# Ranking edges inside a tile of 125: 160 accumulating VectorE operations of one tile, or 40 masks of four tiles summed by TensorE

## The chip, the cores and the metric

The kernel runs on one core of a Trainium2 chip. The metric is the device time of one execution in microseconds (us). Engines are named as the profile names them: PE is TensorE, PEld its weight loads, DVE is VectorE, ACT is ScalarE, POOL is GpSimd, SP is SyncE. A name with a q behind it (PEldq, DVEq) is an instruction of that engine's queue that is no work on data: register arithmetic, a branch, a semaphore.

## What is computed

The program is a chain of four graph layers over 1250 nodes and 20000 edges, each followed by a layer norm. Only its skeleton matters here:

```python
edge_index = jnp.stack([src, dst])
x = _layernorm(x + _L0_gnn_ref(x, edge_index_t, 1250, W, b))        # sums over edges by src
x = _layernorm(x + _L1_gnn_ref(x, edge_index, edge_type_8, ...))    # attention, sums by dst
x = _layernorm(x + _L2_gnn_ref(x, src, dst, deg, ...))              # mean by dst
x = _layernorm(x + _L3_gnn_ref(x, edge_index, edge_type_2, ...))    # two relational layers
return x
```

The sums over edges are made with edges sorted by node. So the kernel first sorts the 20000 edges twice: once by `src`, once by `dst`.

## The kernel before

`sort_edges` is called twice in a row at the start of the program, with `name` `src` and then `dst`, and each call has three stages; every stage ends with a barrier of all engines. The first stage counts and ranks, the second turns counts into positions, the third moves the edges there (and multiplies the basis weights of the last layers beside it). Only the first stage is touched.

In it the edges lie as a table of 125 partitions by 160 columns. A column is a tile of 125 edges, 16 tiles (`GT`) are a group, and there are 10 groups (`G`). The node number is split in a high part of 80 values and a low part of 16 values, and each edge becomes a one-hot row of 96. Four engines' loops work on it:

- `build` (DVE) makes the one-hots of a group, in two operations (L293).
- `turn` (PE) transposes the 16 tiles into `pT` (L322) and multiplies 16 times for the counts, into `pC` (L330).
- ACT copies the transposes to SBUF (L353, two copies a group) and the counts (L356, one).
- `compare` (PE) multiplies each transposed one-hot tile by itself into `pE` (L341). The entry for edges i and j of a tile is the number of halves that they share, so it is 2.0 where both have the same node.
- `rank` (DVE) compares such a tile of 125x125 with 2.0, multiplies by the constant mask `earlier` and sums each row with `accum_out`: for each edge the number of earlier edges of its tile with the same node (L307, once per tile, 160 times).

`pE` holds 16 tiles, one group. The order on each engine is fixed by `lagged`, which writes a step i that runs each work on group i minus its lag: on DVE `build(i)`, then `rank(i-2)`; on PE `turn(i)`, then `compare(i-1)`. `peeled` writes the first steps and what is left at the end out one by one, with constant addresses, and puts the steps between in a hardware loop whose addresses and waits are worked out from a register. The number of steps written out ahead of the loop is 1 plus the greatest lag: 3 on DVE, 2 on PE.

Of the kernel before, what the change touches and what calls it, by code (L numbers as in the profile page):

```python
# [19 lines left out]
F32, BF16, I32 = mybir.dt.float32, mybir.dt.bfloat16, mybir.dt.int32  # L20
ALU, ACT, AX = mybir.AluOpType, mybir.ActivationFunctionType, mybir.AxisListType
# [5 lines left out]
EP, T = 125, 160  # L27
GT = 16
# [8 lines left out]
def stage_semaphores(nc, ctx, name):  # L37

    taken = []

    def give_back():
        nc.clear_and_free_semaphores(taken)
        nc.all_engine_barrier(sem_only=True)  # L43

    ctx.callback(give_back)

    def sem(what):
        taken.append(nc.alloc_semaphore(name=f"{name}_{what}_{nc.next_id()}"))
        return taken[-1]

    return sem


def chain(eng, sem):

    count = [0]

    def link(ins):
        count[0] += 1
        ins.then_inc(sem, 1)  # L60
        eng.wait_ge(sem, count[0])

    return link


def wait(eng, sem, value):

    if isinstance(value, int) and value <= 0:
        return
    eng.wait_ge(sem, value)  # L70


def peeled(eng, n, body, first=1, last=0):

    for i in range(first):
        body(i)
    with eng.Fori(first, n - last) as i:  # L77
        body(i)
    for i in range(n - last, n):
        body(i)  # L80
# [6 lines left out]
def lagged(eng, steps, width, works, last=0):  # L87


    most = max(lag for lag, _ in works)  # L90

    def step(i):
        for u in range(width):
            for lag, work in works:
                back = -((u - lag) // width)
                if not (isinstance(i, int) and i < back):
                    work(i - back, u - lag + back * width)

    peeled(eng, steps, step, first=1 + most // width, last=last)
    for n in range(most):  # L100
        for lag, work in works:
            if n < lag:
                at = steps * width + n - lag
                work(at // width, at % width)
# [132 lines left out]
def sort_edges(nc, name, C, identb, key, packed, extra, pair_block, block_f, sorted_out, basis=None):  # L237
# [7 lines left out]
    with ExitStack() as ctx:  # L245
        sb = lambda n, s, d: ctx.enter_context(nc.sbuf_tensor(f"{name}_{n}", s, d))
# [9 lines left out]
        rankin = sb("rank_in_tile", [EP, T], F32)  # L256
# [2 lines left out]
        small = sb("small", [HI, 8], F32)  # L259
        smalli = sb("small_i", [HI, 2], I32)  # L260
        atleast = sb("pair_at_least", [HI, PAIRS], F32)
        eqtmp = sb("eq_tmp", [EP, 4, EP], F32)
        pos_p, pos_s = sb("pos_partition", [EP, T], F32), sb("pos_slot", [EP, T], F32)
        value = sb("packed_value", [EP, T], F32)

# [1 line left out]
        with ExitStack() as c1:  # L267
            sem = stage_semaphores(nc, c1, name)
            pt = c1.enter_context(nc.psum_tensor(f"{name}_pT", [KO, 2, 8, 128], BF16))
            pc = c1.enter_context(nc.psum_tensor(f"{name}_pC", [HI, GT, LO], F32))  # L270
            pe_ = c1.enter_context(nc.psum_tensor(f"{name}_pE", [EP, 4, 4, 128], F32))
            s_dve = sem("dve_chain")
            onehots_ready = sem("onehots_ready")
            transposed, counted, moved = sem("transposed"), sem("counted"), sem("moved")
            compared, ranked = sem("compared"), sem("ranked")
            block = c1.enter_context(nc.Block())

            G = T // GT

            @block.vector  # L280
            def _(v):
                link = chain(v, s_dve)

                link(nc.vector.tensor_copy(ki[:, :], key))
                link(nc.vector.tensor_single_scalar(ti[:, :], ki[:, :], LB, ALU.logical_shift_right))
                link(nc.vector.tensor_copy(hif[:, :], ti[:, :]))
                link(nc.vector.tensor_single_scalar(ti[:, :], ki[:, :], LO - 1, ALU.bitwise_and))
                link(nc.vector.tensor_copy(lof[:, :], ti[:, :]))

                def build(g, _):  # L290

                    for f, iota, a, n in ((hif, "iota_hi", 0, HI), (lof, "iota_lo", HI, LO)):
                        nc.vector.tensor_tensor(  # L293
                            onehot[:, bass.ds(g * GT, GT), a:a + n],
                            C.f(iota, EP).unsqueeze(1).to_broadcast([EP, GT, n]),
                            f[:, bass.ds(g * GT, GT)].unsqueeze(2).to_broadcast([EP, GT, n]), ALU.is_equal,
                        ).then_inc(onehots_ready, 1)

                def rank(g, _):

                    for u in range(GT):
                        if u % 4 == 0:
                            v.wait_ge(compared, g * 4 + (u // 4 + 1))

                        wait(v, ranked, g * GT + (u - 3))

                        nc.vector.scalar_tensor_tensor(  # L307
                            eqtmp[:, u % 4, :], pe_[:, u // 4, u % 4, 0:EP], 2.0,
                            C.f("earlier", EP)[:, 0:EP], ALU.is_equal, ALU.mult,
                            accum_out=rankin[:, bass.ds(g * GT + u, 1)]).then_inc(ranked, 1)  # L310

                lagged(v, G, 1, [(0, build), (2, rank)])

            @block.tensor
            def _(pe):
                def turn(g, _):

                    pe.wait_ge(onehots_ready, g * 2 + 2)

                    wait(pe, moved, g * 3)  # L320
                    for u in range(GT):
                        ins = nc.tensor.transpose(  # L322
                            pt[:, u // 8, u % 8, 0:EP],
                            onehot[:, bass.ds(g * GT + u, 1), :].rearrange("p a n -> p (a n)"),
                            identb[0:EP, 0:EP])
                        if u % 8 == 7:
                            ins.then_inc(transposed, 1)
                    for u in range(GT):
                        oh = onehot[:, bass.ds(g * GT + u, 1), :].rearrange("p a n -> p (a n)")
                        ins = nc.tensor.matmul(pc[:, u, :], oh[:, 0:HI], oh[:, HI:KO],  # L330
                                               start=True, stop=True)
                    ins.then_inc(counted, 1)

                def compare(g, _):

                    pe.wait_ge(moved, g * 3 + 2)
                    for u in range(GT):
                        if u % 4 == 0:
                            wait(pe, ranked, g * GT + (u + 4 - GT))
                        oh = onehotT[:, bass.ds(g * GT + u, 1), :].rearrange("p a n -> p (a n)")  # L340
                        ins = nc.tensor.matmul(pe_[:, u // 4, u % 4, 0:EP], oh, oh, start=True, stop=True)  # L341
                        if u % 4 == 3:
                            ins.then_inc(compared, 1)

                lagged(pe, G, 1, [(0, turn), (1, compare)])

            @block.scalar
            def _(act):

                with act.Fori(0, G) as g:  # L350
                    for w in range(2):
                        act.wait_ge(transposed, g * 2 + (w + 1))
                        nc.scalar.copy(  # L353
                            onehotT[:, bass.ds(g * GT + w * 8, 8), :], pt[:, w, :, 0:EP]).then_inc(moved, 1)
                    act.wait_ge(counted, g + 1)
                    nc.scalar.copy(cnt[:, :, bass.ds(g * GT, GT)].rearrange("p l t -> p t l"),  # L356
                                   pc[:, :, :]).then_inc(moved, 1)


        with ExitStack() as c1:  # L360
            sem = stage_semaphores(nc, c1, name)
# [98 lines left out]
        with ExitStack() as c1:  # L460
            sem = stage_semaphores(nc, c1, name)
# [1009 lines left out]
def gnn(nc, ins, consts, out):  # L1471
# [8 lines left out]
    with ExitStack() as top:  # L1480
# [16 lines left out]
        with ExitStack() as ctx:  # L1497
# [4 lines left out]
            with ExitStack() as c1:  # L1502
# [14 lines left out]
                def _(v):  # L1517
# [7 lines left out]
            f = lambda n: fld[:, n, :]  # L1525
            SH1, SH2 = 8, 19
            sort_edges(nc, "src", C, identb, f(SRC), [(f(DST), 1 << SH1), (f(REL1), 1 << SH2)], None,
                       pairs["src"][:, :], blocks["src"][:, :], [packed["src"][:, :]], basis[1])
            sort_edges(nc, "dst", C, identb, f(DST), [(f(SRC), 1 << SH1), (f(T8), 1 << SH2)], f(WT),
                       pairs["dst"][:, :], blocks["dst"][:, :], [packed["dst"][:, :], weight[:, :]], basis[0])  # L1530

# [231 lines left out]
```

## Time and profile before

| what | value |
|---|---|
| median of 3 runs | 2698.16 us (2689.44 to 2699.32) |
| span of the profiled execution, first to last instruction | 2541.8 us |
| PE busy | 1969.9 us, 78% |
| DVE busy | 1458.9 us, 57% |
| first stage of the sort by src, first key operation to last rank | 10.7 to 90.6 us |
| the same of the sort by dst | 310.2 to 387.5 us |

The profile gives no other time of its own execution than its span, from the first to the last instruction. The run time is the larger by 156 us, which lie outside the instructions. A difference in the span is therefore read as a difference in the run time. Both stages together are some 157 us of the 2541.8, and what they do to the total is read from inside them: the engines are idle there for other reasons than in the rest.

### The profile page before, as it was taken

The numbers are of one execution on the slowest core, as the hardware profiler recorded it, in microseconds if no ns is written. First come the engines' busy times: TensorE is split into PE (matmuls) and PEld (weight loads), VectorE is DVE, ScalarE is ACT, GpSimd is POOL, SyncE is SP. The second block draws the span as 40 slices with busy tenths as digits, with TensorE's granted clock in tenths as the row PEclk, the third lists the DMA queues.
The fourth block names the chain that finished last, engine by engine and source line by source line (L and its number), as shares of the span: only waits on it lengthen the run. The fifth ranks groups of instructions, "written<-read, shape, count | busy, mean of one in ns | idle before, by whom it ended". The sixth has DMA issues, their size and how long they took to land. (4 is left out here: it accounts for less than half of the span.)

```text
span 2541.8 us, 36616 instructions
## 1 busy us (share of the span) xinstructions
PE 1969.9 (78%) x8289; PEld 1126.0 (44%) x8290; DVE 1458.9 (57%) x3550; ACT 479.5 (19%) x889; POOL 976.5 (38%) x974
## 2 busy tenths in 40 slices
PE   7767695885989998558287775699867998888884
PEld 6633385564545554347144442233333333343331
DVE  5644467675257776687677777444453444204445
ACT  4101130111135554223200002100044000120000
POOL 0000000001047771440078773477700777207773
PEclk9988755998989999755599998899989999999998
DMA  0079700998046663000166670577712777317775
GB/s 16 0 160 212 157 0 21 205 206 214 32 117 193 186 191 74 26 0 0 50 176 172 173 183 28 174 208 210 196 36 95 236 209 207 102 66 206 209 208 143
DMA packets 99747, 336.66 MB, mean 132 GB/s; under 512 B 19744, under 2 KB 20369, under 8 KB 95851
## 3 DMA queue, kind: packets, MB, share of 16 engines
q0 software_dynamic: 71904, 235.41, 33.2%
q1 hardware_dynamic: 24714, 96.39, 14.9%
q10 hardware_dynamic: 3072, 4.20, 0.8%
q8 instruction: 24, 0.39, 0.1%
q14 instruction: 33, 0.26, 0.0%
HBM read 310.83 MB, written 25.10 MB: 132 GB/s over the span
## 5 line engine op out<-in xcount | busy, mean ns | idle before, releaser
L658 PE MATMUL e_pS<-e_rows,e_onehot_ring 128*128 128x512 f32 x1408 | 689.4, 617 | 179.9 <-issue 59.7
L578 POOL DMA_INDIRECT e_rows<-tab_y,e_idx_ring x352 | 334.8, 951 | 332.7 <-ACT e_idx_ring L638 226.1
L658 PEld LDWEIGHTS e_pS<-e_rows,e_onehot_ring 128*128 128x128 f32 x1408 | 246.4, 192 | 480.8 <-issue 404.6
L610 DVE TENSOR_TENSOR acc<-e_pS,acc 128x512 f32 x352 | 242.6, 689 | 377.1 <-PE e_pS L658 373.9
L578 POOL DMA_INDIRECT e_rows<-tab_h,e_idx_ring x176 | 205.0, 1165 | 208.1 <-ACT e_idx_ring L638 158.5
L968 PE MATMUL n_pY<-weights,n_xT_block 128*128 128x512 f32 x560 | 260.1, 615 | 0.0
L1583 POOL DMA_DIRECT2D a_in<-in_L_gnn_a_src x1 | 1.0, 966 | 611.0 <-POOLq L43 611.0
L578 POOL DMA_INDIRECT e_rows<-tab_n,e_idx_ring x176 | 167.7, 953 | 77.2 <-issue 49.9
L717 POOL DMA_INDIRECT e_rows<-tab_q,e_idx_ring x176 | 169.8, 965 | 68.1 <-issue 46.4
L792 PE MATMUL e_pS<-e_rows,e_onehot_f 128*128 128x512 f32 x352 | 166.6, 597 | 0.0
L968 PEld LDWEIGHTS n_pY<-weights,n_xT_block 128*128 128x128 f32 x560 | 107.5, 199 | 118.3 <-issue 118.3
L600 DVE TENSOR_TENSOR e_rows<-e_rows,edge_weights 128x1024 f32<-128x1024 f32 x88 | 108.0, 1227 | 67.1 <-DMA e_rows<-tab_h,e_idx_ring 66.5
L214 PE MATMUL basis_ps<-basis_piece,basis_mix 120*32 120x512 f32 x512 | 81.5, 765 | 77.7 <-DMA basis_piece<-in_L_gnn_basis 77.7
L225 ACT COPY basis_wout<-basis_ps 128x512 f32<-128x512 f32 x64 | 37.5, 585 | 410.7 <-PE basis_ps L214 403.4
L507 PE MATMUL dst_pO<-dst_onehot_s,dst_onehot_p 125*128 125x176 f32 x640 | 107.3, 325 | 6.7 <-DVE dst_onehot_s L494 6.7
L736 DVE TENSOR_TENSOR e_rows<-e_rows,e_pP 128x1024 f32<-128x1024 f32 x88 | 107.3, 1219 | 7.8 <-DMA e_rows<-tab_q,e_idx_ring 7.1
L507 PEld LDWEIGHTS dst_pO<-dst_onehot_s,dst_onehot_p 125*128 125x128 f32 x640 | 97.8, 193 | 26.0 <-DVE dst_onehot_s L494 13.2
L661 PEld LDWEIGHTS e_pN<-edge_weights,e_onehot_ring 128*128 128x128 f32 x352 | 67.7, 192 | 85.8 <-issue 85.8
L761 ACT ACTIVATE e_rows<-e_rows 128x1024 f32<-128x1024 f32 x88 | 93.2, 1059 | 5.7 <-DVE e_rows L736 5.7
L745 DVE TENSOR_TENSOR acc<-e_pS,acc 128x512 f32 x88 | 60.8, 691 | 54.9 <-PE e_pS L792 54.9
L489 DVE TENSOR_SCALAR src_onehot_p<-const_table,src_pos_partition 125x128 f32<-125x128 f32 x160 | 44.7, 280 | 82.5 <-PE src_pO L507 82.3
L638 ACT COPY e_idx_ring<-idx_h 128x8 int32 (+1 forms) x44 | 8.5, 197 | 436.7 <-DMA e_rows<-tab_h,e_idx_ring 236.2
(309 smaller groups left out, 3077.4 us busy)
## 6 DMA issues: line engine op xcount, KB each, us to landing
basis_piece<-in_L_gnn_basis SPq DMA_DIRECT2D x128, 480.0 KB, 11.8
tab_y<-n_y_ring SPq DMA_DIRECT2D x40, 256.0 KB, 2.2
e_rows<-tab_y,e_idx_ring POOLq DMA_INDIRECT x352, 3.7
tab_w<-basis_wout ACTq DMA_DIRECT2D x128, 32.0 KB
w_raw<-in_L_gnn_W SPq DMA_DIRECT2D x3, 1024.0 KB, 10.1
weights<-tab_w SPq DMA_DIRECT2D x3, 1024.0 KB, 5.8
e_rows<-tab_q,e_idx_ring POOLq DMA_INDIRECT x176, 3.7
e_rows<-tab_h,e_idx_ring POOLq DMA_INDIRECT x176, 3.8
```

What stands on the lines that cost most here:

```text
L214: ins = self.nc.tensor.matmul(self.ps[32 * q:32 * q + 32, k * 2 + s, :], self.mix[:, :], self.piece[:, k, f:f + D], start=True, stop=True, ...
L507: ins = nc.tensor.matmul(po[:, n, 0:SLOTS], onp[:, u % RING, :], ons[:, u % RING, n, :], start=first and u == 0, stop=last and u == STEP - 1)
L578: pool.indirect_dma_start(rows[:, q, s, :], None, table, bass.IndirectOffsetOnAxis(idxr[:, half, n:n + 1], 0)).then_inc(got[q], 16)
L600: nc.vector.tensor_tensor(r, r, weight[:, bass.ds(i * 16 + u * 2, 2), 0:H].unsqueeze(3).to_broadcast([P, 2, H, DH]), ALU.mult).then_inc(we ...
L610: nc.vector.tensor_tensor(a, pS[:, u % 4, :], a, ALU.add).then_inc(added, 1)
L658: ins = nc.tensor.matmul(pS[:, u % 4, :], ohr[:, u % 4, s, :], rows[:, u, s, :], start=s == 0, stop=s == 1)
L661: ins = nc.tensor.matmul(pN[:, u % 4, 0:ns], ohr[:, u % 4, s, :], weight[:, bass.ds(i * 16 + (u * 2 + s), 1), :].rearrange("p a h -> p (a ...
L717: pool.indirect_dma_start(rows[:, q, s, :], None, q_table, bass.IndirectOffsetOnAxis(idxr[:, half, n:n + 1], 0)).then_inc(got[q], 16)
L736: nc.vector.tensor_tensor(rows[:, u, :, :], rows[:, u, :, :], pP[:, u % 2, :, :], ALU.add).then_inc(summand, 1)
L761: nc.scalar.activation(rows[:, u, :, :], rows[:, u, :, :], ACT.Relu).then_inc(relued, 1)
L792: ins = nc.tensor.matmul(pS[:, u % 2, :], ohf[:, u, s, :], rows[:, u, s, :], start=s == 0, stop=s == 1)
L968: ins = nc.tensor.matmul(py[:, k, w, :], xt[:, k, c, :], weights[w][0][:, c, :], start=c == 0, stop=c == 3)
```

## The change

`rank` on DVE is replaced by two works. `match` on DVE compares a window of four tiles at once (125x500) and writes the masked comparison (0.0 or 1.0) as two-byte numbers into `same`, without summing. A new `rank` on PE multiplies each of the four masks by a column of ones: the mask is the stationary operand, the ones are the moving one, and the result, one column of 125 sums, goes to a new PSUM tile `pR`. After the last group one DVE copy brings `pR` to `rankin`. The step on PE is now `turn(i)`, `compare(i-1)`, `rank(i-2)`; on DVE `build(i)`, `match(i-2)`. The greatest lag on PE goes from 1 to 2. Lines shift: L322, L330 and L341 of before are L324, L332 and L343 of the changed kernel; L307 is the DVE comparison in both.

```diff
-        eqtmp = sb("eq_tmp", [EP, 4, EP], F32)
+        same = sb("same_and_later", [EP, 4, 4, EP], BF16)
+        ones = sb("ones", [EP, 1], BF16)
...
+            pr = c1.enter_context(nc.psum_tensor(f"{name}_pR", [EP, T], F32))
...
+                link(nc.vector.memset(ones[:, :], 1.0))
...
-                def rank(g, _):
-
-                    for u in range(GT):
-                        if u % 4 == 0:
-                            v.wait_ge(compared, g * 4 + (u // 4 + 1))
-
-                        wait(v, ranked, g * GT + (u - 3))
-
+                def match(g, _):
+
+                    for w in range(4):
+                        v.wait_ge(compared, g * 4 + (w + 1))
+                        wait(v, ranked, g * 4 + (w - 3))
                         nc.vector.scalar_tensor_tensor(
-                            eqtmp[:, u % 4, :], pe_[:, u // 4, u % 4, 0:EP], 2.0,
-                            C.f("earlier", EP)[:, 0:EP], ALU.is_equal, ALU.mult,
-                            accum_out=rankin[:, bass.ds(g * GT + u, 1)]).then_inc(ranked, 1)
-
-                lagged(v, G, 1, [(0, build), (2, rank)])
+                            same[:, w, :, :], pe_[:, w, :, 0:EP], 2.0,
+                            C.f("earlier", EP)[:, 0:EP].unsqueeze(1).to_broadcast([EP, 4, EP]),
+                            ALU.is_equal, ALU.mult).then_inc(matched, 1)
+
+                lagged(v, G, 1, [(0, build), (2, match)])
+                v.wait_ge(ranked, 4 * G)
+                nc.vector.tensor_copy(rankin[:, :], pr[:, :])
...
-                            wait(pe, ranked, g * GT + (u + 4 - GT))
+                            wait(pe, matched, g * 4 + (u // 4 - 3))
...
-                lagged(pe, G, 1, [(0, turn), (1, compare)])
+                def rank(g, _):
+
+                    for w in range(4):
+                        pe.wait_ge(matched, g * 4 + (w + 1))
+                        for q in range(4):
+                            ins = nc.tensor.matmul(pr[:, bass.ds(g * GT + (w * 4 + q), 1)], same[:, w, q, :], ones[:, :],
+                                                   start=True, stop=True, skip_group_check=True)
+                        ins.then_inc(ranked, 1)
+
+                lagged(pe, G, 1, [(0, turn), (1, compare), (2, rank)])
```

What PE issues ahead of its loop in the sort by src, before the change (`ISA` is an instruction of the queue that sets registers or waits, the figures at the end are the shape of the result):

```order
L322 MATMUL src_pT<-identb,src_onehot 96x125 x16
L330 MATMUL src_pC<-src_onehot 80x16 x16
L322 MATMUL src_pT<-identb,src_onehot 96x125 x16
L330 MATMUL src_pC<-src_onehot 80x16 x16
L341 MATMUL src_pE<-src_onehotT 125x125 x16
L77 UNCONDITIONAL_BRANCH
```

The same place after the change:

```order
L324 MATMUL src_pT<-identb,src_onehot 96x125 x16
L332 MATMUL src_pC<-src_onehot 80x16 x16
L324 MATMUL src_pT<-identb,src_onehot 96x125 x16
L332 MATMUL src_pC<-src_onehot 80x16 x16
L343 MATMUL src_pE<-src_onehotT 125x125 x16
L324 MATMUL src_pT<-identb,src_onehot 96x125 x16
L332 MATMUL src_pC<-src_onehot 80x16 x16
L343 MATMUL src_pE<-src_onehotT 125x125 x16
L352 MATMUL src_pR<-src_ones,src_same_and_later 125x1 x16
L77 UNCONDITIONAL_BRANCH
```

A whole step, with its `compare` and the first `rank`, has moved out of PE's loop, so that the loop runs 7 times and no longer 8.

The end of PE's loop and what follows it, before the change (each matmul in the loop has an `ISA` of its own ahead of it):

```order
L341 ISA
L341 MATMUL src_pE<-src_onehotT 125x125
L77 REGISTER_ALU
L77 COMPARE_AND_BRANCH
L341 MATMUL src_pE<-src_onehotT 125x125 x16
```

The same place after the change, with the first window of the new `rank`; three more windows like it, each with a `REGISTER_ALU` ahead, stand between the two pieces:

```order
L343 ISA
L343 MATMUL src_pE<-src_onehotT 125x125
L350 ISA
L352 ISA
L352 MATMUL src_pR<-src_ones,src_same_and_later 125x1
...
L77 REGISTER_ALU
L77 COMPARE_AND_BRANCH
L343 MATMUL src_pE<-src_onehotT 125x125 x16
L352 MATMUL src_pR<-src_ones,src_same_and_later 125x1 x32
```

PE's loop body has grown by 16 matmuls, 16 `ISA` of their own and 4 register instructions, and behind the loop stand 32 matmuls more.

## Rows read from the trace of the kernel before

**Rows 1.** The first line of the page of the profile.

```profile
span 2541.8 us, 36616 instructions
```

**Rows 2.** Windows of one loop step: src, dst; x counts instructions, then PEclk, DMA.

```profile
31.98:39.70 7.72, 7.26 (x48) 6.77 (x49) 5.39 (x35) 3.75 (x4) 0.00 (x0) 1.00 0.00 0
328.90:336.71 7.81, 7.31 (x48) 6.80 (x49) 5.68 (x37) 2.57 (x3) 0.00 (x0) 0.50 0.00 1
```

**Rows 3.** Waits, 0 to 95 us: us in total, times, longest.

```profile
DVE src_eq_tmp L307 <- PE src_pE L341: 23.5, 9, 5.0
...
PE src_pT L322 <- ACT src_cnt L356: 2.4, 2, 2.1
...
PEld src_pE L341 <- DVE src_eq_tmp L307: 0.3, 1, 0.3
```

**Rows 4.** Timeline of PE, 20 to 40 us: start, length, operation, count.

```profile
20.64 1.22 PE L330 MATMUL src_pC<-src_onehot 125*80 125x16 bf16 x16
21.71 1.95 PE L341 MATMUL src_pE<-src_onehotT 96*125 96x125 bf16 x16
23.95 2.53 PE L322 MATMUL src_pT<-identb,src_onehot 125*96 125x125 bf16 x16 [0.29 <-ACT src_cnt L356]
...
31.99 2.43 PE L322 MATMUL src_pT<-identb,src_onehot 125*96 125x125 bf16 x16 [0.39 <-issue]
34.23 2.30 PE L330 MATMUL src_pC<-src_onehot 125*80 x16
36.64 2.72 PE L341 MATMUL src_pE<-src_onehotT 96*125 x16
39.70 0.60 PE L322 MATMUL src_pT<-identb,src_onehot 125*96 125x125 bf16 x3 [0.34 <-issue]
```

**Rows 5.** Timeline of all engines, 60 to 125 us: last step, end of stage.

```profile
78.38 2.43 PE L322 MATMUL src_pT<-identb,src_onehot 125*96 125x125 bf16 x16 [0.34 <-issue]
...
85.73 1.35 PEld L341 LDWEIGHTS src_pE<-src_onehotT 96*125 96x125 bf16 x12 [0.16 <-issue]
...
90.55 0.08 DVE L307 DVE_READ_ACCUMULATOR src_eq_tmp<-src_pE,const_table 125x1 f32 x1
91.37 0.06 DVE L376 MEMSET src_small<- 80x1 f32 x1 [0.73 <-PEq L43]
```

**Rows 6.** Source views, 31.9 to 82.9 us: PE's queue; ns min/median/max, starts.

```profile
L330 PEldq FUSED_REGOPS  x112: 55/55/55, 34.1 to 82.6; - x112
...
L341 PEldq FUSED_REGOPS  x96: 55/64/69, 36.5 to 77.6; - x96
...
L77 PEldq COMPARE_BRANCH  x6: 207/208/213, 39.1 to 77.8; - x6
```

**Rows 7.** Timeline of PE, 300 to 392 us, and the last rank of dst.

```profile
321.69 1.89 PE L322 MATMUL dst_pT<-identb,dst_onehot 125*96 125x125 bf16 x16
...
328.90 2.44 PE L322 MATMUL dst_pT<-identb,dst_onehot 125*96 125x125 bf16 x16 [0.34 <-issue]
...
375.29 2.42 PE L322 MATMUL dst_pT<-identb,dst_onehot 125*96 125x125 bf16 x16 [0.35 <-issue]
...
387.43 0.08 DVE L307 DVE_READ_ACCUMULATOR dst_eq_tmp<-dst_pE,const_table 125x1 f32 x1
```

**Rows 8.** Groups by form on DVE, 31.98 to 78.37 us: busy us, mean ns.

```profile
L307 DVE SCALAR_TENSOR_TENSOR src_eq_tmp<-src_pE,const_table 125x125 f32<-125x125 f32 x97 | 22.0, 285 | 12.2 <-PE src_pE L341 12.2
...
L293 DVE TENSOR_TENSOR src_onehot<-const_table,src_hi_f 125x1280 f32 x6 | 9.0, 1493 | 1.5 <-issue 1.5
...
L293 DVE TENSOR_TENSOR src_onehot<-const_table,src_lo_f 125x256 f32 x6 | 2.5, 419 | 0.0
```

**Rows 9.** The page's costliest groups: a DVE operation on 512 columns of PSUM.

```profile
L745 DVE TENSOR_TENSOR acc<-e_pS,acc 128x512 f32 x88 | 60.8, 691 | 54.9 <-PE e_pS L792 54.9
```

**Rows 10.** Timeline of ACT's third group, 0 to 60 us.

```profile
28.75 0.59 ACT L356 COPY src_cnt<-src_pC 80x256 f32 x1 [0.22 <-PE src_pC L330]
```

**Rows 11.** Timeline of PE, 85 to 135 us: the second stage's loop.

```profile
120.95 5.16 PE L451 MATMUL src_pG<-src_prefix_parts,src_onehotT 80*125 x32 [0.33 <-issue]
```

More of the change, by code:

```diff
@@ L274, in sort_edges @@
             transposed, counted, moved = sem("transposed"), sem("counted"), sem("moved")
-            compared, ranked = sem("compared"), sem("ranked")
+            compared, matched, ranked = sem("compared"), sem("matched"), sem("ranked")
+            pr = c1.enter_context(nc.psum_tensor(f"{name}_pR", [EP, T], F32))
             block = c1.enter_context(nc.Block())
```

## The prediction

> **What bounds the stage now.** The chain on the page's foot covers only the program's last microseconds, so I read the two ranking stages from inside. First the windows of one loop step. In the sort by src a step takes 7.72 us, of which PE is busy 7.26 and DVE 5.39 [rows 2]. The step repeats: `turn(3)` starts at 31.99 and `turn(9)` at 78.38, which is 46.39 us for six steps, 7.73 each [rows 4, 5]. Then the waits: DVE waits 23.5 us for PE's `pE`, while PE's loads wait 0.3 us for DVE in the whole stage [rows 3]. So PE sets the pace and DVE, from which the change takes work, is the engine that waits.
>
> Next, what holds PE. Ahead of the loop, with constant addresses, the 16 count matmuls start at 20.64 and the next work at 21.71: 1.07 us, 67 ns each. In the loop the same 16 take from 34.23 to 36.64, 2.41 us to the next work, and the 16 transposes from 31.99 to 34.23: 2.24 us, 140 ns each [rows 4]. The difference stands in PE's queue: ahead of each of these matmuls one register instruction of 55 ns, and at the end of each step a branch of 208 ns [rows 6]. The clock is not it: in the sort by dst the granted clock is 0.50, the lower of the two levels (1.2 GHz), in src it is 1.00 (2.4 GHz), and the step takes 7.81 us against 7.72 [rows 2]. So PE's queue bounds the loop by the number of its instructions, whatever their size. A matmul of one column costs there what one of 125 does.
>
> **What the change does to a loop step.** It removes 16 DVE operations of 227 ns each (22.0 us over 97), 3.6 us, and adds four of 500 columns out of PSUM. The nearest row is a DVE operation on 512 columns of PSUM, 691 ns [rows 8, 9]; a bit less, 0.68 us, gives 2.7 us. With `build` (1.49 and 0.42) DVE then has 4.6 us in a step. I cost these edits at nothing: they lie beside PE's work both before and after. This cover goes only if DVE needed more than PE's step.
>
> It adds to PE 16 matmuls, 16 register instructions of their own and four waits. Neither is in the trace, so I bound their cost. From below: 16 pairs at the loop's 140 ns, 2.24 us. From above: `compare` is built alike, 16 pairs with four waits; from its start at 36.64 to the next `turn` at 39.70 are 3.06 us, and without the branch (0.21) 2.85, in which `turn`'s own two waits are counted too [rows 4, 6]. The new pairs have one changing address like the transposes, so I go between, 2.6 us. PE's idle time in a step, 0.46 us [rows 2], offers no cover, since its queue is at work then. **A step becomes 7.73 + 2.6 = 10.33 us.**
>
> Here the Trainium skill speaks of another price. "TensorE: Matmul & The Clock Gate", section "Back-to-back issue gap", gives about 81 ns for a sustained pair of weight load and matmul of 128 columns. By that figure the new `rank` would take 16 x 81 ns = 1.3 us, a step 9.0 us, and the total would rise by some 17 us and not by 35. The trace agrees with it roughly for the matmuls that are written out (67 ns) and not for those in the loop (140 ns).
>
> **New waits.** `match(i-2)` waits on `compare(i-2)`, and, window by window, on `rank(i-3)`, both of PE's previous step. PE needs it only for `rank(i-2)`, behind `turn(i)` and `compare(i-1)`, some 7.3 us later; DVE needs 2.7 us for it and 1.9 for the next `build`. Behind a late `match` on DVE only that `build` is queued, and PE's `turn` would wait for it; it has some 5 us to spare. `compare` now waits on `matched` of the group before, which comes earlier than `ranked` did.
>
> **The step that leaves the loop.** With a lag of 2 PE writes out three steps and loops over seven. In src `turn(2)` starts at 23.95 either way, released by ACT [rows 4]. Written out, it costs 1.7 us for transposes (105 ns each, an estimate between the 67 and 140 ns above) and 1.07 for counts, `compare(1)` 1.9 [rows 4], `rank(0)` 16 x 67 ns = 1.1, the loop's entry 0.3: `turn(3)` at about 30.0 where it was 31.99. ACT's copies for that group ended at 29.3 [rows 10], so they don't hold it. In dst: 321.69 + 6.0 = 327.7, where it was 328.90 [rows 7].
>
> **The end of the stage.** Before, PE left its loop at 85.73, 7.35 us after `turn(9)`, and DVE's last rank came at 90.63; 0.7 us later the next stage began [rows 5]. Now that step takes 7.35 + 2.6 = 9.95 us. Behind it come `compare(9)` written out, 1.9; the first window of `rank(8)`, 0.3, for which the first window of `match(9)` waits; four windows of `match`, 0.6 us from one to the next, 2.4; the last window of `rank(9)` with its release, 0.6; and the copy of `pR` into `rankin`, 0.3 (160 columns, less than the 419 ns of 256 [rows 8]). Together 5.5 us.
>
> **The sum, against the profiled span.** Src: 30.0 + 6 x 10.33 = 92.0 for `turn(9)`, + 9.95 + 5.5 = 107.4, against 90.6: +16.8 us. Dst: 327.7 + 62.0 + 9.95 + 5.5 = 405.1, against 387.5 [rows 7]: +17.6. The two `memset`s of `ones` add 0.1 each. Sum +34.6, say +35 us on a span of 2541.8 [rows 1]. The later stages only move back: each begins behind a barrier. That their granted clock might differ is not priced; the range has room for it. The runs' median, 2698.16, holds 156 us outside the span that the change doesn't touch, so the forecast is 2698 + 35 = **2733 us**. With the bounds of 2.24 and 2.85 us for the new `rank`, over 14 steps of the two loops, its own range is +30 to +38 us, 2728 to 2737.
>
> **Rivals.**
> - *The new matmuls go at the array's pace, not the queue's* (10%). A weight load whose address is constant might take no turn in the queue worth speaking of; then 16 x 67 ns and the waits come to 1.2 us. 14 steps x 1.4 us less: +15 us, 2713. For it: the written-out rate. Against: both kinds of matmul in the loop take 140 ns or more from one to the next, whatever the shape, and the order shows an `ISA` ahead of each new matmul. The skill's figure above would land here.
> - *The new matmuls cost more* (12%). The loop of the second stage needs 5.16 us for 32 pairs, 161 ns each [rows 11]. With that and 0.6 us of waits, 3.2 us: +8 us over the forecast, 2741.
> - *A new ring of waits* (3%). `same` holds one group, so `match` and `rank` wait for one another. If PE had to stand through `match`, 2.7 us a step on 14 steps: +38 us more, 2771. It decides only once DVE's 4.6 us no longer fit beside PE's 7.7.
> - *Hidden work* (4%). If PE's queue had slack and the new matmuls cost under 1 us a step, the total would stay within 13 us of before.
> - *Faster* (2%). If PE's pace were set by DVE's round trip, 0.9 us less DVE work a step (3.6 against 2.7) would give back up to 14 us over 16 steps: 2684. It decides if PE stands waiting on DVE for more than 2.6 us in a step; the trace shows 0.3 us in a whole stage [rows 3].
>
> My forecast has 69%. Within 0.5% means 13.5 us, about what a measurement of this kernel can tell from no change. Part of the first rival falls inside it, so: slower 0.92, same 0.06, faster 0.02. The range reaches down past the first rival and up past the second: 2711 to 2748.
>
> **What the changed profile would show.** Seven loop steps in each sort of 10.3 us (10.0 to 10.6 by my bounds); the new `pR` matmuls about 140 ns apart, with a register instruction ahead of each; DVE busy in a step down to about 4.6 us and its wait for `pE` grown; the first stage ending at about 107 and 405 less the shift of the first sort, that is 422 in the new trace. Steps of 9 us would prove the first rival, and PE idle in front of `rank`, released by DVE's `match`, the ring of waits. The forecast is wrong at its root if PE's step stays near 7.7 us.

## The result, and the profile after

| | before | after |
|---|---|---|
| median run | 2698.74 us (4 runs) | 2724.8 us (4 runs, 2718.95 to 2729.0) |
| ratio | | 1.0118, 95% interval 1.0095 to 1.0142 |
| first stage, src: first key operation to the `small` memset behind the barrier | 80.7 us | 95.9 us |
| first stage, dst | 78.1 us | 94.1 us |

The change makes the kernel slower: by 26 us between the medians, by 1.2% in the recorded ratio. A recorded ratio, here and below, comes with its interval and is not the quotient of the two medians (1.0097 here); on 2699 us it stands for 32 us (26 to 38). The two ranking stages of the profiles grow by 15.2 + 16.0 = 31.2 us.

PE's timeline of the changed kernel, 0 to 130 us in the sort by src (start, length, operation, count), answers to [rows 4] and [rows 5]:

```profile
23.60 1.88 PE L324 MATMUL src_pT<-identb,src_onehot 125*96 125x125 bf16 x16 [0.28 <-ACT src_cnt L367]
...
28.09 1.81 PE L352 MATMUL src_pR<-src_ones,src_same_and_later 125*125 125x1 bf16 x16
29.76 1.90 PE L324 MATMUL src_pT<-identb,src_onehot 125*96 125x125 bf16 x16
...
38.89 2.51 PE L324 MATMUL src_pT<-identb,src_onehot 125*96 125x125 bf16 x16 [0.47 <-issue]
...
49.24 2.42 PE L324 MATMUL src_pT<-identb,src_onehot 125*96 125x125 bf16 x16 [0.45 <-issue]
51.46 2.29 PE L332 MATMUL src_pC<-src_onehot 125*80 x16
53.88 2.75 PE L343 MATMUL src_pE<-src_onehotT 96*125 x16
56.51 2.46 PE L352 MATMUL src_pR<-src_ones,src_same_and_later 125*125 125x1 bf16 x16
...
89.99 2.40 PE L324 MATMUL src_pT<-identb,src_onehot 125*96 125x125 bf16 x16 [0.48 <-issue]
...
99.77 1.94 PE L343 MATMUL src_pE<-src_onehotT 96*125 96x125 bf16 x16
101.50 3.71 PE L352 MATMUL src_pR<-src_ones,src_same_and_later 125*125 125x1 bf16 x32
```

Read it by the starts of `turn` (L324). From the step that starts at 38.89 to the one at 89.99 are five steps in 51.10 us, 10.22 each, where they took 7.73. The 16 new matmuls of one column last 2.46 us, little more than the 16 count matmuls (2.29). No gap stands in front of them. The first loop step, 29.76 to 38.89, is cheaper, 9.13 us.

Windows of one step in each sort, after (length, then busy time and instruction count of PE, PEld, DVE, ACT and POOL; PEclk, DMA share, GB/s), against [rows 2]:

```profile
49.24:59.45 10.21, 9.60 (x65) 9.05 (x65) 4.31 (x7) 3.75 (x4) 0.00 (x0) 1.00 0.00 0
363.48:373.69 10.21, 9.63 (x64) 9.05 (x65) 4.30 (x7) 2.57 (x3) 0.00 (x0) 0.50 0.00 0
```

DVE is down from 5.39 to 4.31 us of work in a step, and the step is longer all the same. The granted clock is at its higher level (2.4 GHz) in one and at its lower (1.2 GHz) in the other; both take 10.21 us.

The waits of 0 to 110 us, after, answer to [rows 3] (total, times, longest):

```profile
DVE src_same_and_later L307 <- PE src_pR L352: 45.0, 9, 7.6
...
DVE src_same_and_later L307 <- PE src_pE L343: 5.0, 1, 5.0
...
DVE src_rank_in_tile L314 <- PE src_pR L352: 0.7, 1, 0.7
```

DVE's wait has doubled, from 23.5 to 50 us, and changed its name: the masks of a group now wait until `rank` has read those of the group before. No row of this view has PE waiting for a mask. The source view of the new matmuls, whole span (ns min/median/max), against [rows 6]:

```profile
L352 PEldq FUSED_REGOPS  x224: 46/46/51, 35.7 to 413.6; - x112
```

In the loops each new matmul has its register instruction ahead of it, 46 ns long.

Why is the first loop step cheap? The source view of the transposes (26 to 31.5 us) shows when the queue's own register instructions for them started; below it is the same view before the change, in the middle of the loop (39 to 42 us):

```profile
L324 PEldq FUSED_REGOPS  x16: 55/55/61, 28.5 to 30.5; - x16
```

```profile
L322 PEldq FUSED_REGOPS  x16: 55/55/60, 39.6 to 41.7; - x16
```

After the written-out step the queue starts on the transposes at 28.5, while the first of them runs only at 29.76: it is 1.2 us ahead of the array. In the loop before, it starts at 39.6 and the first transpose at 39.70, so it has no lead. The first loop step is cheaper by 1.1 us, about that lead.

### The profile page after: what moved, and what is told of

It is laid out like the page before. It is cut to its first block and busy times, and to the rows that moved or that the text cites. A ratio compares the mean times of both kernels' runs of the same rounds, so it can differ in the third digit from the quotient of the medians.

```text
span 2722.0 us, 36614 instructions
## 1 busy us (share of the span) xinstructions
PE 2068.7 (76%) x8609; PEld 1203.9 (44%) x8610; DVE 1437.4 (53%) x2994; ACT 480.8 (18%) x889; POOL 996.4 (37%) x974
## 5 line engine op out<-in xcount | busy, mean ns | idle before, releaser
L669 PE MATMUL e_pS<-e_rows,e_onehot_ring 128*128 128x512 f32 x1408 | 747.3, 673 | 244.7 <-DVE e_onehot_ring L603 134.3
L669 PEld LDWEIGHTS e_pS<-e_rows,e_onehot_ring 128*128 128x128 f32 x1408 | 281.2, 213 | 559.0 <-issue 397.5
L621 DVE TENSOR_TENSOR acc<-e_pS,acc 128x512 f32 x352 | 242.8, 690 | 514.1 <-DMA tab_y<-n_y_ring 160.9
L589 POOL DMA_INDIRECT e_rows<-tab_y,e_idx_ring x352 | 340.9, 969 | 394.7 <-ACT e_idx_ring L649 224.2
L589 POOL DMA_INDIRECT e_rows<-tab_h,e_idx_ring x176 | 211.1, 1200 | 217.3 <-ACT e_idx_ring L649 156.3
L214 PE MATMUL basis_ps<-basis_piece,basis_mix 120*32 120x512 f32 x512 | 76.0, 718 | 73.7 <-DMA basis_piece<-in_L_gnn_basis 73.7
L803 PEld LDWEIGHTS e_pS<-e_rows,e_onehot_f 128*128 128x128 f32 x352 | 68.2, 195 | 54.1 <-issue 46.5
L793 PE MATMUL e_pP<-p_high,e_onehotT 128*128 x176 | 79.9, 454 | 14.9 <-ACT e_onehotT L766 7.1
L968 PE MATMUL n_pT<-const_table,n_x_block 128*128 128x128 f32 x200 | 37.4, 318 | 69.9 <-DVE n_x_block L858 63.5
```

What stands on the lines that cost most here:

```text
L214: ins = self.nc.tensor.matmul(self.ps[32 * q:32 * q + 32, k * 2 + s, :], self.mix[:, :], self.piece[:, k, f:f + D], start=True, stop=True, ...
L589: pool.indirect_dma_start(rows[:, q, s, :], None, table, bass.IndirectOffsetOnAxis(idxr[:, half, n:n + 1], 0)).then_inc(got[q], 16)
L621: nc.vector.tensor_tensor(a, pS[:, u % 4, :], a, ALU.add).then_inc(added, 1)
L669: ins = nc.tensor.matmul(pS[:, u % 4, :], ohr[:, u % 4, s, :], rows[:, u, s, :], start=s == 0, stop=s == 1)
L793: ins = nc.tensor.matmul(pP[:, u % 2, s, :], ohT[:, u % 2, s, :], flat(p_parts[n][:, bass.ds(b, 1), :]), start=n == 0, stop=n == 1)
L803: ins = nc.tensor.matmul(pS[:, u % 2, :], ohf[:, u, s, :], rows[:, u, s, :], start=s == 0, stop=s == 1)
```

## The experiments

All comparisons below are with the kernel before on the same chip, whose median there was 2544.7 us in the first set (the first, second and fourth experiment below) and 2544.2 in the second.

### The same matmuls with VectorE left alone

```diff
# on the kernel before; `ones`, its memset, `pr` and `ones_in` are added as well
...
-                lagged(pe, G, 1, [(0, turn), (1, compare)])
+                def unused(g, _):
+
+                    for u in range(GT):
+                        nc.tensor.matmul(pr[:, bass.ds(g * GT + u, 1)], identb[0:EP, 0:EP], ones[:, :],
+                                         start=True, stop=True, skip_group_check=True)
+
+                pe.wait_ge(ones_in, 1)
+                lagged(pe, G, 1, [(0, turn), (1, compare), (2, unused)])
```

> The kernel before, with its 160 VectorE rank operations kept, and 16 more matmuls of one column per group on TensorE at the place of the new rank, whose results nobody reads (their stationary operand is the identity, so they wait for nothing). Theory (TensorE's queue paces the loop, 10.2 us a step after the change against 7.7 before): a step becomes 7.7 + 16 x 0.13 = 9.8 us with VectorE untouched, both ranking stages together grow by some 25 to 28 us, the total by 1.0% (1.009 to 1.011). Rival A (the cost of the change comes from the new waits between VectorE and TensorE): little, under 8 us, since there are no such waits here. Rival B (the array's pace, 67 ns a matmul): 1.1 us a step, 15 us in all, ratio 1.005.

Measured: 2567.1 us, ratio 1.0112 (1.0073 to 1.0152). PE's timeline of this kernel:

```profile
58.20 2.41 PE L326 MATMUL src_pT<-identb,src_onehot 125*96 125x125 bf16 x16 [0.45 <-issue]
...
87.57 2.42 PE L326 MATMUL src_pT<-identb,src_onehot 125*96 125x125 bf16 x16 [0.45 <-issue]
```

Three steps in 29.37 us, 9.79 each: the 16 matmuls add 2.06 us, 129 ns apiece, although nobody reads them and nothing waits. The stages are 24.9 us longer (92.8 and 90.8 us). So most of the change's 31 us is the matmuls' own place in PE's order. The rest, 10.22 less 9.79 or 0.4 us a step, is put down to the four waits; no run adds them alone. Taking 160 operations off DVE (and giving it 40) gives nothing back. Both rivals fall: the new waits alone would have left this kernel near before, and the array's pace would have given 1.1 us a step.

### Constant result columns

The changed kernel with a `pR` of one group, whose columns have constant addresses:

```diff
# on the changed kernel
...
-            pr = c1.enter_context(nc.psum_tensor(f"{name}_pR", [EP, T], F32))
+            pr = c1.enter_context(nc.psum_tensor(f"{name}_pR", [EP, GT], F32))
...
-                lagged(v, G, 1, [(0, build), (2, match)])
-                v.wait_ge(ranked, 4 * G)
-                nc.vector.tensor_copy(rankin[:, :], pr[:, :])
+                def keep(g, _):
+                    v.wait_ge(ranked, g * 4 + 4)
+                    nc.vector.tensor_copy(rankin[:, bass.ds(g * GT, GT)], pr[:, :]).then_inc(kept, 1)
+
+                lagged(v, G, 1, [(0, build), (3, keep), (2, match)])
...
+                    wait(pe, kept, g)
...
-                            ins = nc.tensor.matmul(pr[:, bass.ds(g * GT + (w * 4 + q), 1)], same[:, w, q, :], ones[:, :],
+                            ins = nc.tensor.matmul(pr[:, w * 4 + q:w * 4 + q + 1], same[:, w, q, :], ones[:, :],
```

> The changed kernel, but the 16 result columns of rank have constant addresses (a PSUM tile for one group, copied to rankin by one small VectorE operation per group), so the register instruction ahead of each of the 16 new matmuls goes. Theory (instructions in TensorE's queue): 16 x 46 ns = 0.74 us a step less, one more wait of 0.05: a step of 9.5 us instead of 10.2, total 9 to 10 us under the changed kernel, ratio to before 1.006 to 1.008. Rival (weight loads and matmuls themselves set the pace, the register instructions run beside them): step and total as in the changed kernel, 10.2 us and ratio 1.012.

Measured: 2555.1 us, ratio 1.0036 (1.0019 to 1.0053). PE's timeline:

```profile
62.58 1.90 PE L326 MATMUL src_pT<-identb,src_onehot 125*96 125x125 bf16 x16
...
69.18 1.86 PE L355 MATMUL src_pR<-src_ones,src_same_and_later 125*125 125x1 bf16 x16
70.90 1.90 PE L326 MATMUL src_pT<-identb,src_onehot 125*96 125x125 bf16 x16
```

A step is 8.32 us, not the expected 9.5. Removing 16 register instructions of 46 ns (0.74 us) took 1.9 us off the step. The direction was right and my price was far too small; the rival (no change) falls as well. The transposes behind the new matmuls also start 105 ns apart here (1.69 us for 16) instead of 140. PE's queue had got ahead of the array while `rank` ran, as the source view of the transposes (61 to 64.5 us) shows, and it lives on that lead for the next 16:

```profile
L326 PEldq FUSED_REGOPS  x16: 55/55/60, 61.8 to 63.9; - x16
```

Their register instructions start at 61.8, 0.8 us ahead of the first transpose. The two stages last 171.1 us, 18.9 less than in the changed kernel. That is less than 14 steps would give. In part it is because VectorE now waits for a group's sums (`keep`) before it makes the next masks: behind the loop PE waits twice for them, 0.94 us each.

### Unread matmuls with constant addresses

Here the question is put directly. The edit is the first experiment's, with one difference:

```diff
-                        nc.tensor.matmul(pr[:, bass.ds(g * GT + u, 1)], identb[0:EP, 0:EP], ones[:, :],
+                        nc.tensor.matmul(pr[:, u:u + 1], identb[0:EP, 0:EP], ones[:, :],
```

> As the kernel before with 16 unread matmuls a group, but their result columns have constant addresses, so they have no register instruction ahead of them. The constant column of the changed kernel took 116 ns off each new pair, where the register instruction itself lasts 46. Theory A (a pair whose address hangs on a register costs the queue some 130 ns as a whole, one with constant addresses nearly nothing): a step of 7.8 to 8.1 us instead of 9.8, total near the kernel before, ratio 1.000 to 1.003. Theory B (only the 46 ns of the register instruction go, the pair itself costs the queue 83 ns): a step of 9.05 us, some 18 us more than before, ratio 1.006 to 1.008.

Measured: 2543.9 us, ratio 0.9991 (0.9970 to 1.0011). PE's timeline of this kernel:

```profile
52.18 1.90 PE L326 MATMUL src_pT<-identb,src_onehot 125*96 125x125 bf16 x16
53.87 1.73 PE L334 MATMUL src_pC<-src_onehot 125*80 x16
55.72 2.76 PE L345 MATMUL src_pE<-src_onehotT 96*125 x16
58.27 1.81 PE L352 MATMUL src_pR<-src_ones,identb 125*125 125x1 bf16 x16
59.94 1.90 PE L326 MATMUL src_pT<-identb,src_onehot 125*96 125x125 bf16 x16
```

This step takes 7.76 us. Over six loop steps of src the mean is 7.79, over five of dst 7.75 (the first at a granted clock of 1.00, the second at 0.50), against 7.73 of the kernel before, with 16 matmuls and weight loads more in it. PE shows busy with them for 1.7 us, and the work around them closes up by as much: the transposes take 1.69 us to the counts where they took 2.24, the counts 1.85 to the next work where they took 2.41, and `compare` 2.55 where it took 3.06 with the loop's end behind it. The queue's side of it, in the source views of `compare` (55 to 59 us), the branch (55 to 60) and the transposes (58 to 62):

```profile
L345 PEldq FUSED_REGOPS  x16: 55/64/69, 55.6 to 58.0; - x16
L77 PEldq COMPARE_BRANCH  x1: 213/213/213, 58.3 to 58.3; - x1
L326 PEldq FUSED_REGOPS  x16: 55/55/60, 58.7 to 60.8; - x16
```

The 16 constant pairs lie in the queue between the last register instruction of `compare` at 58.0 and the branch at 58.3. In the kernel before, where nothing lies there, that stretch is 38.9 to 39.1. So the queue hands all 16 on in about 0.1 us, while the array is at them until 59.94.

Theory A holds and B (9.05 us) falls. In a loop that the queue paces, these 16 pairs with constant addresses are as good as free (at most 0.06 us a step), and with a column address out of a register they cost 129 ns each, though the register instruction shows only 46 of them.

The Trainium skill, "TensorE: Matmul & The Clock Gate", section "Wait — 56ns, not 53.3ns?", says that with hardware decoding turned on, by a debug switch of the runtime, matmuls and weight loads are issued straight to the engine without the sequencer's microcode; with it off the page gives some 62 ns a matmul. The trace agrees with the first for the 16 pairs with constant addresses, which take the queue about 0.1 us together. How the switch stood is not on record.

### TensorE's loop written out, before and after

```diff
# the same on both kernels; (2, rank) stands in the list of the changed one
-def lagged(eng, steps, width, works, last=0):
+def lagged(eng, steps, width, works, last=0, written_out=False):
...
-    peeled(eng, steps, step, first=1 + most // width, last=last)
+    if written_out:
+        for i in range(steps):
+            step(i)
+    else:
+        peeled(eng, steps, step, first=1 + most // width, last=last)
...
-                lagged(pe, G, 1, [(0, turn), (1, compare)])
+                lagged(pe, G, 1, [(0, turn), (1, compare)], written_out=True)
```

> The kernel before, with TensorE's ranking loop written out step by step (all addresses constant), nothing else. Theory: TensorE needs 4.7 us for a group (1.7 + 1.1 + 1.9) and no longer sets the pace; VectorE does with 5.5 to 5.8 us (build 1.9, 16 ranks of 0.21 to 0.23). A step falls from 7.7 to 5.7 us, 8 steps and 2 sorts: 30 to 34 us less, ratio 0.988. Rival (array or weight loads bound it): no change, ratio 1.000.

> The changed kernel with TensorE's ranking loop written out in the same way. Theory: TensorE needs 4.7 + 1.7 = 6.3 us for a group (1.7 us for rank as in the step ahead of its loop) and still sets the pace, since VectorE needs 4.3: a step of 6.3 instead of 10.2 us, 7 steps and 2 sorts, 52 to 55 us less than the changed kernel, ratio to before 0.990, and slower than the kernel before written out by 4 to 8 us. Rival (array or weight loads bound it): no change, ratio 1.012.

Measured: before written out 2506.8 us, ratio 0.9860 (0.9819 to 0.9902); after written out 2514.3 us, ratio 0.9893 (0.9847 to 0.9939). Windows of two steps of the first:

```profile
47.75:52.84 5.09, 4.70 (x49) 4.52 (x49) 5.09 (x35) 3.66 (x4) 0.00 (x0) 1.00 0.01 3
52.84:57.96 5.12, 4.73 (x48) 4.54 (x48) 5.12 (x35) 3.65 (x4) 0.00 (x0) 1.00 0.00 0
```

DVE is busy from end to end. This is what a stage bound by VectorE looks like, and the kernel before did not look so. In the early steps ACT's copies release `turn`, 4.98 us apart. The steps of 5.0 to 5.1 us are shorter than the 5.7 that I expected, so the stages lose 41 us and not 30 to 34: I had 0.21 to 0.23 us for each of VectorE's 16 ranks, and beside `build` (1.9 us) they take 0.20. PE's timeline of the changed kernel, written out:

```profile
60.69 1.90 PE L328 MATMUL src_pT<-identb,src_onehot 125*96 125x125 bf16 x16
...
66.86 1.90 PE L328 MATMUL src_pT<-identb,src_onehot 125*96 125x125 bf16 x16
```

Here the step is 6.17 us of unbroken PE work (6.3 expected), while DVE waits 18.2 us for `pR` between 20 and 75 us. So the two stages together last 117.6 us (before, written out), 137.0 (after, written out), 158.8 (before) and 190.0 (after). The array or weight loads did not bound either loop. And the change loses without the register instructions too: the stages say by 19 us, the run medians by 7.5. The two ratios have overlapping intervals, so the runs alone do not show it; the stages do. The later parts hold the same instructions in both, and they last 2114.1 and 2106.0 us from the end of the second stage of dst. In the seven other profiles with spans under 2600 us that stretch lies between 2093.5 and 2118.4 us, in no order of the edits, so it scatters by more than the difference in question.

### A version that beats both

The second stage's loop has two changing addresses per pair, 161 ns apart [rows 11]. It was written out as well:

```diff
# on the kernel before with its ranking loop written out
-                peeled(pe, T // GT // 2, step)
+                for g in range(T // GT // 2):
+                    step(g)
```

> The kernel before with TensorE's ranking loop and its loop of the second stage (pG) written out, no change on VectorE. Theory: beside the 38 us of the written-out ranking loop, a double step of the second stage falls from 5.5 us to what VectorE needs, 3.4 to 3.7 (two times 1.66 and a wait), four of them in each sort: 14 to 17 us more, ratio 0.979 to 0.982. Rival (that stage is bound by VectorE or by the weight loads of 125 columns at 105 ns, 3.4 us for 32, plus the latency between them): under 6 us more, ratio 0.984 or above.

Measured: 2494.3 us, ratio 0.9784 (0.9748 to 0.9819), 50 us less than before. Its PE timeline in the second stage, and then its waits of 85 to 110 us (total, times, longest):

```profile
84.68 14.21 PE L455 MATMUL src_pG<-src_prefix_parts,src_onehotT 80*125 80x32 bf16 x128 [6.45 <-DVE src_prefix_parts L402]
99.04 3.67 PE L455 MATMUL src_pG<-src_prefix_parts,src_onehotT 80*125 80x32 bf16 x32 [0.15 <-DVE src_gather_tmp L411]
```

```profile
DVE src_gather_tmp L411 <- DVE src_rank_to_tile L416: 3.2, 8, 0.6
DVE src_gather_tmp L411 <- PE src_pG L455: 2.1, 2, 1.8
```

DVE's timeline (84 to 106 us), the same operation one double step apart:

```profile
98.29 0.69 DVE L411 TENSOR_TENSOR src_gather_tmp<-src_pG,src_onehot 125x512 f32<-125x512 f32 x1 [0.54 <-DVE src_rank_to_tile L416]
...
102.12 0.69 DVE L411 TENSOR_TENSOR src_gather_tmp<-src_pG,src_onehot 125x512 f32<-125x512 f32 x1 [0.54 <-DVE src_rank_to_tile L416]
```

The first 128 matmuls take 3.6 us for each 32 instead of 5.5, and DVE's waits for `pG` are 2.1 us, where they were 11.2. Behind the first of them, 1.8 us, DVE waits 0.3 us for PE and 3.2 us for its own `src_rank_to_tile`: now VectorE sets the pace, and its double step settles at 3.83 us (from 98.29 to 102.12), above the expected 3.4 to 3.7. The second stage of src ends 36.2 us after it began (69.4 to 105.6), before 42.1: 5.9 us in each sort by the traces, 12.5 us by the run medians of the two sets. That is short of the 14 to 17 expected; the ratio lies at the edge of the expected 0.979 to 0.982. The rival, under 6 us in all, falls.

### Both kernels once more

> The changed kernel unaltered, on the same chip as the other runs of this set, to tell what belongs to the change from what belongs to the chip. The ranking stages last 31 us longer than before in the first profile (95.9 and 94.1 us against 80.7 and 78.1), the run time grew by 26. Theory (nothing but these stages changes): ratio 1.010 to 1.013, the stages to within 0.5 us as in the first profile whatever the span. Rival (later stages give some of it back): stages as before, total growth clearly under 31 us in a profile of the same chip.

> The kernel before unaltered, one profile on this chip. Its first profile had a span of 2541.8 us beside runs of 2698. If 156 us lay outside the span, the run's time is again some 150 us over its span. If it was another chip or state, time and span agree to a few us, and the ranking stages last 80.7 and 78.1 us as in the first profile.

The changed kernel: 2577.7 us, ratio 1.0122 (1.0090 to 1.0153), its ranking stages 95.9 and 94.1 us. The span of its profile is 38.1 us longer than that of the kernel before (next below), the stages 31.2. So the rival, that later stages give some of it back, has no support here. The kernel before: a run of 2543.25 us whose page begins

```profile
span 2540.9 us, 36616 instructions
```

with stages of 80.7 and 78.1 us. Time outside the span is 2.3 us and not 156 (1.7 in the profiled run of the changed kernel at 2723.74 us). So the first profile, 2541.8 us, does not belong to the runs near 2699; it fits the chips of the experiments, where this kernel takes 2544. That the first runs were on another chip is likely and not shown, since the record names the chip of the experiments (12 and 9) alone. The ranking stages don't see the difference: in the changed kernel they agree to 0.1 us between the span of 2722.0 and that of 2579.0. Of these 143 us, 141 lie behind the second stage of dst.

## Why the prediction was right, and where its sizes were off

- **What bounds the stage.** Right. PE's queue sets the pace, DVE waits. The unread matmuls (25 us of 31 with DVE's work left as it was) and the written-out loops (41 us less) show it.
- **"Whatever their size", and "the number of its instructions".** Too coarse. One column costs what 125 do, as said. But what counts is not any instruction: pairs with constant addresses are next to free (7.79 and 7.75 us a step against 7.73), those with a register address cost 129 ns. It came out right because every new pair in the loop had one.
- **The new `rank`, 2.6 us a step.** Measured 10.22 - 7.73 = 2.5, of which 2.06 are the 16 pairs and 0.4, by what is left, the four waits. It lies between my bounds of 2.24 and 2.85. The pairs alone cost less than my lower bound.
- **DVE costed at nothing.** Right: 4.31 us in a step (4.6 forecast).
- **The waits.** `match` is released by `rank`, as said, and PE never stands waiting for its masks in the loop. I forecast that the wait for `pE` would grow; it is the wait for `pR` that did.
- **The step out of the loop.** `turn(3)` at 29.76 (30.0 forecast), which is luck in part: the stage began 0.34 us earlier, and from `turn(2)` it took 6.16 us where I had 6.05. The first `rank` took 1.67 us and not 1.1, for I priced its 125-column weights by the count matmuls' 67 ns, whose weights have 80 columns; `compare` took 1.74 and not 1.9, and the loop's entry of 0.3 doesn't show. Not seen: the first loop step takes 9.13 us, 1.1 less than the others, because the queue enters the loop 1.2 us ahead of the array.
- **The end.** 5.8 us from 99.77 to 105.58 (5.5 forecast).
- **The sum.** +31.2 us in the stages, +34.6 forecast. The term mis-sized most is the loops': `turn(9)` came at 89.99 and not 92.0, through the cheap first step (1.2), 0.1 us in each of the five others and the 0.24 by which `turn(3)` was early. The forecast, 2733, missed the median by 8 us; 2724.8 lies in the range, a little under my own case's 2728 to 2737. By the stages (31.2 us) and by the ratio (32 us) that case, +30 to +38, holds.
- **Where the reading was wrong.** The 156 us "outside the instructions", which stand in the prediction and ahead of it, don't exist. The sum was not harmed: the stages last the same at both speeds, and only the base of 2698 came from the slower runs.
- **The rivals.** The array's pace (10%) did not come true in the loop: 129 ns a pair and not 67. It describes the changed kernel written out, at 105 ns a pair and not 67. With constant columns in the loop the 16 pairs and the waits cost even less than its 1.2 us, 0.6 (8.32 - 7.73). The 81 ns of the Trainium skill ("TensorE: Matmul & The Clock Gate", section "Back-to-back issue gap") is given for matmuls of 128 columns; the trace has 105 ns for the new pairs of one column where they are written out, and 129 in the loop.
- **Stages and whole runs.** The medians grew by 26 us in the first runs and 33.5 in the last set, the stages by 31.2. The recorded ratios say 32 and 31 us (1.0118 and 1.0122), and in every experiment the difference of the edited stages lies inside the interval of the ratio. So no run shows that later stages give or take some. What makes up the 0.4 us beside the 16 pairs stays open.

## What to carry to other kernels

Find out whether the engine from which work is taken is the one that waits. Here VectorE waited, so three quarters of its rank operations could go for no gain, and their replacement on TensorE cost its full price. In a hardware loop of small matmuls look at the queue's register instructions first: put the changing part of an address in as few matmuls as possible, or write the loop out. Writing one loop out was worth 38 us here, with no change to the work.

## What was unexpected of the hardware

A register instruction ahead of a matmul shows 46 ns, but removing the changing address saved 127 ns a pair (9.79 to 7.76 us for 16, in the unread pairs). A lead that PE's queue gains over 16 constant matmuls (1.2 us by its register instructions) is spent on the work behind them: the next 16 run at 105 ns instead of 140. And the same kernel ran at 2544 and at 2699 us, while the ranking stages of the changed one were equal to 0.1 us at both speeds.
